# A fused LayerNorm, attention and diffusion kernel on one core: sums by banks at the end, degrees and y earlier at the seam

## The reference

```python
h = jnp.maximum(_layernorm(x, axis=-1), 0.0)
deg = jnp.clip(adj.sum(axis=1), 1.0)
dis = deg ** (-0.5)
diffusion = (dis[:, None] * adj * dis[None, :]) @ h - h
norms = jnp.maximum(jnp.linalg.norm(h, axis=-1), COS_EPS)
sim = h @ h.T / (norms[:, None] * norms[None, :])
attn = jax.nn.softmax(beta * sim * adj, axis=1)
out = x + diffusion + jax.nn.sigmoid(alpha) * (attn @ h - h)
```

## Time and profile before

| | |
|---|---|
| median of 3 runs | 1929.85 us (1928.91 to 1930.41) |
| the profiled execution's own time | 1930.2 us |
| its span, first to last instruction | 1928.3 us |
| mean granted TensorE clock | 0.995 of full |
| TensorE matmul busy | 1829.0 us, 95% of the span |
| VectorE, ScalarE, GpSimd busy | 1222.3, 1307.6 and 1269.9 us |
| the seam: TensorE idle from the last attention sum to the first diffusion matmul | 9.35 us |
| the end: last diffusion matmul at 1918.1, end of the span at 1928.3 | 10.2 us |

### The profile page before, as it was taken

How to read it: one execution, slowest core, us unless ns; L and a number is a source line. 1 busy time by engine, 2 the same in 40 slices (tenths; PEclk the granted TensorE clock), 3 DMA queues, 4 the chain that set the end, 5 groups by cost and what they waited for, 6 DMA issues and landing times.

```text
span 1928.3 us, 44739 instructions
## 1 busy us (share of the span) xinstructions
PE 1829.0 (95%) x19602; PEld 1410.2 (73%) x19602; DVE 1222.3 (63%) x1376; ACT 1307.6 (68%) x1262; POOL 1269.9 (66%) x792
## 2 busy tenths in 40 slices
PE   0499999999999999999999999999997999999997
PEld 0366777777777777777777777777776888888887
DVE  6877787778778777877777787787775210111110
ACT  7688898889889888988988898898886000000000
POOL 3099999999999999999999999999881000000000
PEclk9999999999999999999999999999998999999999
DMA  9639887777888876788887678888217754645520
GB/s 177 96 64 140 102 107 104 91 99 95 101 105 104 103 99 91 100 99 107 100 109 101 89 100 100 106 100 109 61 45 302 246 188 160 207 165 196 176 99 12
DMA packets 188311, 229.38 MB, mean 119 GB/s; under 512 B 9300, under 2 KB 164948, under 8 KB 183380
## 3 DMA queue, kind: packets, MB, share of 16 engines
q0 software_dynamic: 135168, 67.13, 44.8%
q1 hardware_dynamic: 24916, 144.71, 20.2%
q10 hardware_dynamic: 28032, 14.69, 3.0%
HBM read 352.32 MB, written 75.50 MB: 222 GB/s over the span
## 4 chain that ended last, share of the span: by engine, by line
PE 86%; POOL 6%; ACT 3%; DVE 2%; issue 2%; DMA 0%; SPq 0%; POOLq 0%; DVEq 0%; ACTq 0%
PE cos_ps L656 30%; PE cos_ps L715 12%; PE top_ps L715 12%; PE top_ps L686 11%; PE top_ps L690 11%; PE top_ps L688 10%; POOL ustage L275 6%; ACT arena L317 1%; ACT xe L341 0%; PE cos_ps L642 0%; DMA asb<-x_in 0%; DVE ustage L504 0%; POOL hlo L266 0%; DVE ptmp L475 0%; ACT xe L325 0%
## 5 line engine op out<-in xcount | busy, mean ns | idle before, releaser
L275 POOL TENSOR_TENSOR ustage<-xe,ustage 128x1024 f16<-128x1024 f32 x512 | 1095.7, 2144 | 153.0 <-ACT xe L398 148.4
L570 DVE TENSOR_TENSOR xe<-cos_ps,arena 128x1024 f32<-128x1024 f32 x512 | 626.9, 1224 | 286.4 <-PE cos_ps L656 185.0
L394 ACT ACTIVATE ustage<-xe,ebias,ab 128x1024 f16<-128x1024 f32 x512 | 635.4, 1241 | 132.2 <-DVE xe L570 130.8
L686 PE MATMUL top_ps<-h,ustage 128*128 128x129 f16 x4096 | 719.9, 220 | 3.9 <-POOL ustage L275 3.9
L690 PE MATMUL top_ps<-h,ustage 128*128 128x129 f16 x4096 | 719.8, 220 | 0.0
L688 PE MATMUL top_ps<-hlo,ustage 128*128 128x128 f16 x4096 | 719.2, 219 | 0.0
L398 ACT ACTIVATE xe<-xe,ebias,ab 128x1024 f32<-128x1024 f32 x512 | 628.5, 1228 | 3.3 <-POOL ustage L275 2.2
L686 PEld LDWEIGHTS top_ps<-h,ustage 128*128 128x128 f16 x4096 | 401.0, 98 | 72.3 <-POOL ustage L275 12.2
L688 PEld LDWEIGHTS top_ps<-hlo,ustage 128*128 128x128 f16 x4096 | 401.0, 98 | 57.0
L690 PEld LDWEIGHTS top_ps<-h,ustage 128*128 128x128 f16 x4096 | 401.1, 98 | 0.0
L545 DVE TENSOR_REDUCE top_ps<-arena 128x8 f32<-128x1024 uint16 x256 | 311.7, 1217 | 0.0
(11 more groups left out here) (89 smaller groups left out, 1017.7 us busy)
## 6 DMA issues: line engine op xcount, KB each, us to landing
arena<-adj_in_dram POOLq DMA_DIRECT2D x256, 256.0 KB, 8.5
at_scratch<-arena SPq DMA_DIRECT2D x128, 512.0 KB, 3.1
arena<-at_scratch SPq DMA_DIRECT2D x26, 2048.0 KB, 8.6
xe<-at_scratch SPq DMA_DIRECT2D x6, 2048.0 KB, 8.6
h_scratch<-arena SPq DMA_DIRECT2D x4, 1024.0 KB, 7.6
arena<-h_scratch SPq DMA_DIRECT2D x1, 4096.0 KB, 13.4
ustage<-h_scratch ACTq DMA_DIRECT2D x16, 256.0 KB, 8.3
ptmp<-x_in ACTq DMA_DIRECT2D x64, 64.0 KB, 7.4
```

What stands on the lines that cost most here:

```text
L275: nc.gpsimd.tensor_tensor(elo[:, n % ES, :], ef[:, n % XS, :], ehi[:, n % ES, :], ALU.subtract).then_inc(elo_done, 1)
L394: nc.scalar.activation(ehi[:, n % ES, :], xm[:, n % XS, :], ACT.Exp, bias=ebias[:, 0:1], scale=ab[:, 1:2]).then_inc(ehi_done, 1)
L570: nc.vector.tensor_tensor(xm[:, n % XS, :], cos_ps[:, n % 2, :], at8[:, m % W, :, n % B], ALU.mult).then_inc(x_done, 1)
L686: nc.tensor.matmul(top_ps[:, bank, col:col + P + 1], head, h1[:, s, 0:P + 1], start=(first and t % 3 == 0), stop=final, skip_group_check=True)
```

## The change

Five edits, in the kernel's own order:

1. VectorE's row sums run ahead of their units. The first 16 units take 12 pieces in place of 8 (also after units 2, 6, 10, 14), and from then on each piece comes eight units earlier than before. sum_bytes comes after unit 54 of a panel, not 62.
2. degrees() stands ahead of sums(UNITS - 6), not sums(UNITS - 1). VectorE clips straight from PSUM (clip_deg, four operations) after its last masked().
3. ScalarE's order at the seam: the root and the eight y groups now stand ahead of the last panel's copy_acc. y32 moves from ustage to ptmp and has two buffers, not four.
4. h_again comes back in two halves of 2 MB, into two row slots as these fall free (after chunks 29 and 30), not in one of 4 MB after the last row sum. The slots of the second phase are renumbered: chunk 0 goes to the one that chunk 31's rows leave, chunks 3 and 4 wait for y groups 4 and 8.
5. In the last chunk of each panel TensorE goes bank by bank (2 output tiles by 16 tiles of y), and counts each bank done (tiles_done). VectorE adds each bank as it comes (4 operations), signals ScalarE's queue after every second bank, and the queue stores a half panel (4 DMAs) each time.

```diff
--- before.py
+++ after.py
@@ -85,7 +85,6 @@
         gate = sb("gate", [P, 1], fp32)
         gate_tmp = sb("gate_tmp", [P, 2], fp32)
         neg_1_gate = sb("neg_1_gate", [P, 1], fp32)
-        deg = sb("deg", [P, TILES], fp32)
...
@@ -130,9 +129,11 @@
         elo = ustage[:, 2048:4096].bitcast(fp16).rearrange("p (s i) -> p s i", s=ES)
 
         y = [uT_hi[:, :].rearrange("p (s k) -> p s k", k=2 * P), uT_lo[:, :].rearrange("p (s k) -> p s k", k=2 * P)]
-        y32 = ustage[:, :].rearrange("p (g i) -> p g i", g=4)
-        h_again = arena[:, 2 * 4096:4 * 4096].rearrange("p (s d) -> p s d", d=P)
-        slots = [arena[:, 4096:8192], arena[:, 0:4096], xe[:, :], arena[:, 8192:12288], arena[:, 12288:16384]]
+        y32 = ptmp[:, :].rearrange("p (g i) -> p g i", g=2)
+
+        h_again = [arena[:, 4096:8192].rearrange("p (s d) -> p s d", d=P),
+                   arena[:, 12288:16384].rearrange("p (s d) -> p s d", d=P)]
+        slots = [arena[:, 8192:12288], arena[:, 0:4096], xe[:, :], arena[:, 4096:8192], arena[:, 12288:16384]]
         slot8 = [s.bitcast(fp8).rearrange("p (w i b) -> p w i b", w=W, b=B) for s in slots]
         slotw = [s.bitcast(u32) for s in slots]
         SL = len(slots)
@@ -185,7 +186,8 @@
         deg_ready = sem("deg_ready")
         deg_root = sem("deg_root")
         dis_ready = sem("dis_ready")
-        h_back = sem("h_back")
+        h_back = [sem(f"h_back{g}") for g in range(2)]
+        tiles_done = sem("tiles_done")
         y_scaled = sem("y_scaled")
         y_ready = sem("y_ready")
         at_loaded = [sem(f"at_loaded{s}") for s in range(SL)]
@@ -212,17 +214,23 @@
                 sp.dma_start(h_dram[:, g * GW:(g + 1) * GW],
                              h32[:, 16 * g:16 * (g + 1), :].rearrange("p s d -> p (s d)")).then_inc(h_kept[g], 16)
 
+            def h_stored(half):
+                sp.wait_ge(h_kept[2 * half], 16)
+                sp.wait_ge(h_kept[2 * half + 1], 16)
+
             for m in range(BLOCKS):
                 w = m % W
                 sp.wait_ge(at_ready, m + 1)
                 sp.dma_start(at_dram[m // W, :, 1024 * w:1024 * (w + 1)], at_words[:, w, :]).then_inc(at_stored[w], 16)
-
+                if m // W in (CHUNKS - 3, CHUNKS - 2) and w == W - 1:
+
+                    half = m // W - (CHUNKS - 3)
+                    sp.wait_ge(rows_summed, 8 * (m // W + 1))
+                    h_stored(half)
+                    sp.dma_start(h_again[half].rearrange("p s d -> p (s d)"),
+                                 h_dram[:, 4096 * half:4096 * (half + 1)]).then_inc(h_back[half], 16)
 
             sp.wait_ge(rows_summed, 8 * CHUNKS)
-            for g in range(CH):
-                sp.wait_ge(h_kept[g], 16)
-            sp.dma_start(h_again.rearrange("p s d -> p (s d)"), h_dram).then_inc(h_back, 16)
-
             for w in range(W):
                 sp.wait_ge(at_stored[w], 16 * CHUNKS)
             for k in range(CHUNKS):
@@ -230,11 +238,15 @@
                     sp.wait_ge(x_done, UNITS)
                 elif k == 2:
                     sp.wait_ge(elo_done, UNITS)
-                elif k == 3:
-
-                    sp.wait_ge(y_scaled, PANELS)
+                elif k >= 3 and k < SL:
+
+                    sp.wait_ge(y_scaled, 4 * (k - 2))
                 if k >= SL:
-                    sp.wait_ge(at_used, k - SL + 1)
+                    before = k - SL
+                    if before % CH == CH - 1:
+                        sp.wait_ge(tiles_done, PT // 2 * (before // CH + 1))
+                    else:
+                        sp.wait_ge(at_used, (CH - 1) * (before // CH) + before % CH + 1)
                 sp.dma_start(slotw[k % SL], at_dram[k]).then_inc(at_loaded[k % SL], 16)
 
         @block.gpsimd
@@ -397,9 +409,8 @@
                     act.wait_ge(elo_done, n - XS + 1)
                 nc.scalar.activation(ef[:, n % XS, :], xm[:, n % XS, :], ACT.Exp, bias=ebias[:, 0:1],
                                      scale=ab[:, 1:2]).then_inc(ef_done, 1)
-            copy_acc(PANELS - 1)
-
-            act.wait_ge(deg_ready, 1)
+
+            act.wait_ge(deg_ready, Q)
             nc.scalar.activation(vb[:, :], va[:, :], ACT.Sqrt).then_inc(deg_root, 1)
 
             def load_base(panel):
@@ -411,23 +422,26 @@
                         act.dma_start(o2[C * q:C * (q + 1), panel % 2, CH * w:CH * (w + 1), :], x_again_v[b, w0 + w, q]
                                       ).then_inc(base_loaded[panel % 2], 16)
 
-            act.wait_ge(h_back, 16)
             act.wait_ge(dis_ready, 1)
             for g in range(PANELS):
-                if g >= 4:
-                    act.wait_ge(y_ready, g - 3)
-                for s in range(PT):
-                    last = nc.scalar.activation(y32[:, g % 4, s * P:(s + 1) * P], h_again[:, g * PT + s, :], ACT.Copy,
-                                                scale=dis[:, g * PT + s:g * PT + s + 1])
+                if g % 4 == 0:
+                    act.wait_ge(h_back[g // 4], 16)
+                if g >= 2:
+                    act.wait_ge(y_ready, g - 1)
+                for t in range(PT):
+                    s = g * PT + t
+                    last = nc.scalar.activation(y32[:, g % 2, t * P:(t + 1) * P], h_again[s // 32][:, s % 32, :], ACT.Copy,
+                                                scale=dis[:, s:s + 1])
                 last.then_inc(y_scaled, 1)
+            copy_acc(PANELS - 1)
 
             act.wait_ge(y_ready, PANELS)
             load_base(0)
             load_base(1)
             for panel in range(PANELS):
-                act.wait_ge(out_ready, panel + 1)
                 w0, b = panel_of(panel)
                 for w in range(2):
+                    act.wait_ge(out_ready, 2 * panel + w + 1)
                     for q in range(Q):
                         act.dma_start(out_v[b, w0 + w, q], o2[C * q:C * (q + 1), panel % 2, CH * w:CH * (w + 1), :]
                                       ).then_inc(out_stored[panel % 2], 16)
@@ -555,11 +569,11 @@
                                         in_=bytesums.rearrange("p (ch a h) -> p a ch h", ch=CH, h=2),
                                         axis=AX.XY, op=ALU.add).then_inc(rowsums_ready, 1)
 
-            def copy_deg():
+            def clip_deg():
                 dve.wait_ge(deg_done, 1)
                 for q in range(Q):
-                    last = nc.vector.tensor_copy(deg[C * q:C * (q + 1), :], deg_ps[C * q:C * (q + 1), q, :])
-                link(last)
+                    nc.vector.tensor_scalar(va[C * q:C * (q + 1), :], deg_ps[C * q:C * (q + 1), q, :], 1.0 / EIGHT, 1.0,
+                                            ALU.mult, ALU.max).then_inc(deg_ready, 1)
 
             def masked(n):
                 m = n // B
@@ -575,28 +589,26 @@
             dve.wait_ge(hlo_ready, 8)
             turn(0)
             copy_uT(3)
-            sum_rows(0, 0)
-            for n in range(UNITS):
-                masked(n)
+
+            piece = 0
+            for n in range(-1, UNITS):
+                if n >= 0:
+                    masked(n)
                 if n % B == 1 and n // B + 1 < BLOCKS:
                     turn(n // B + 1)
-                elif n % B == 3 and n + 1 < UNITS:
-                    sum_rows((n + 1) // 16, 2 * ((n + 1) % 16 // B))
-                elif n % B == 0:
-                    sum_rows(n // 16, 2 * (n % 16 // B) + 1)
-                if n % TILES == TILES - 2:
+                elif (n % B in (0, 3) or n in (2, 6, 10, 14)) and piece < 8 * CHUNKS:
+                    sum_rows(piece // 8, piece % 8)
+                    piece += 1
+                if n % TILES == TILES - 10:
                     sum_bytes(n // TILES)
-
-            copy_deg()
-            link(nc.vector.tensor_scalar(vc[:, :], deg[:, :], 1.0 / EIGHT, None, ALU.mult))
-            nc.vector.tensor_scalar(va[:, :], vc[:, :], 1.0, None, ALU.max).then_inc(deg_ready, 1)
+            clip_deg()
             dve.wait_ge(deg_root, 1)
             refine_root(va[:, :], vb[:, :], vc[:, :])
             nc.vector.reciprocal(dis[:, :], vb[:, :]).then_inc(dis_ready, 1)
             for g in range(PANELS):
                 dve.wait_ge(y_scaled, g + 1)
                 yg = y[g // 4][:, (g % 4) * PT:(g % 4 + 1) * PT, :]
-                y32g = y32[:, g % 4, :].rearrange("p (s d) -> p s d", d=P)
+                y32g = y32[:, g % 2, :].rearrange("p (s d) -> p s d", d=P)
                 link(nc.vector.tensor_copy(yg[:, :, 0:P], y32g))
                 nc.vector.tensor_tensor(yg[:, :, P:2 * P], y32g, yg[:, :, 0:P], ALU.subtract).then_inc(y_ready, 1)
             dve.wait_ge(acc_copied, PANELS)
@@ -613,17 +625,19 @@
                     last = nc.vector.scalar_tensor_tensor(out=o[:, t, :], in0=asb[:, u, 0:P], scalar=gz[:, u:u + 1],
                                                           in1=o[:, t, :], op0=ALU.mult, op1=ALU.add)
                 link(last)
-                dve.wait_ge(at_used, CH * (panel + 1))
-                for part in range(2):
```

(55 more changed lines are left out.)

## The result

The changed kernel takes 1921.04 us (median of 5 runs, 1919.42 to 1921.91) against 1929.85 (5 runs, 1928.65 to 1930.41): ratio 0.9954, interval 0.9939 to 0.9968, so 0.3 to 0.6% faster. Forecast were 1921.2 us, and 8.7 us of gain, in a range of 1919.0 to 1924.3. The profiled execution took 1921.04 us with a span of 1919.1, 9.2 us less than the span before.

The account below looks back on a forecast made before the run. TensorE was taken to bound the kernel except at prologue, seam and end. End 5.0 plus seam 3.7 gave 8.7 us off the 1929.85 median: 1921.2 us, range 1919.0 to 1924.3 for 8 in 10.

Parts of the forecast that it names:

- The end: Behind the last matmul: four sum operations left (gain 3.11 us) and four stores left (gain 1.88), 5.0 us in all.
- The seam: Between attention and diffusion: table load right behind the last exponential, first diffusion matmul at 1465.16 not 1468.84, gain 3.68 us.
- The table load: ScalarE at the seam: load at 1457.02, no 1.4 us drain counted; rival of a wait for exponentials, 3 of the 16%.
- The clock: First diffusion panel: clock falls again, same price (2.11 us before) within a microsecond; rival that the clock is kept, 12%.
- The loop: Attention loop: VectorE waits 2.1 us for chunk 2, covered with 0.4 us to spare; cost 0, bounds 0 and 1.5.
- The order of the matmuls: Each panel's last chunk: bank order costs nothing, bound 27 ns each; rival that same-bank matmuls wait, 30 us slower, 3%.
- Edit 4 at nothing: Reloading h in two halves costs nothing; only at_scratch's stores stand behind them in SP's list, each with 10.6 us of room.

Follow-up runs that it names:

- the run with UNITS - 4: Changed kernel with the degrees' matmuls ahead of sums(UNITS - 4), behind the last cosines, not at UNITS - 6: 1918.86 us, ratio 0.9944.
- the run with the degrees last: Changed kernel with the degrees' matmuls back ahead of the last unit's sums (UNITS - 1): 1921.91 us, ratio 0.9956.
- the fill: Changed kernel with 64 unread matmuls of 128 columns between attention and diffusion: 1918.97 us, ratio 0.9943; with degrees at UNITS - 4 and two store queues too, 1916.32 us.

## Why the prediction was right, point by point

- *The total.* The medians lie 8.81 us apart, 8.7 were forecast. That the time itself was met to 0.2 us is in part luck: single runs of the changed kernel spread over 2.5 us, by causes for which the sum has no term (below), and the two profiles lie 9.2 us apart. What holds is that both terms came at their size, each by itself.
- *The end, 5.0 us.* Right by its steps: 1.25 us of sums (the row says 1.25) and four stores. 5.16 in the profile; with edit 5 alone, ratio 0.9975, 0.9974 expected.
- *The seam, 3.68 us.* Right: 3.76 in the profile, 3.77 in the attention's length without edit 5. Every step on the path was within 0.1 us. What the sum left untold is how it divides: degrees() at its new place gives 1.0 net, because the matmuls hold masked(511) by 1.7 us; the run with UNITS - 4 gives these 1.63 back. I had the price right and did not ask whether a free place was near.
- *The table load.* I counted it as one block behind the last exponential. It was right here because clip_deg was done first (not under ef, where the prediction puts it, but 0.3 us before ef starts); the run with the degrees last showed that the load does not wait for them. The drain of about 1.4 us that the Trainium skill ("ScalarE: Activation LUTs", What ACT_TABLE_LOAD costs) adds is not seen in any run: in the changed kernel the load starts at the 1457.00 at which the last exponential ends, and Sqrt starts 0.02 us behind the load. By the page's figure the first diffusion matmul would have come 1.4 us later than it did.
- *The clock.* The price came as forecast, 57.72 - 55.89 = 1.83 us against 2.11. Windows of the changed kernel, with the granted clock behind the five busy times:

```profile
1463.00:1464.00 1.00, 0.00 (x0) 0.00 (x0) 0.97 (x2) 1.00 (x4) 0.00 (x0) 1.00 1.09 426
1464.00:1465.00 1.00, 0.00 (x0) 0.00 (x0) 0.94 (x1) 1.00 (x5) 0.00 (x0) 1.00 0.85 328
1465.00:1466.00 1.00, 0.92 (x6) 0.78 (x7) 0.68 (x1) 1.00 (x4) 0.00 (x0) 0.70 1.04 442
1466.00:1467.00 1.00, 1.00 (x7) 0.71 (x5) 0.97 (x2) 1.00 (x5) 0.00 (x0) 0.50 0.54 229
...
1468.00:1469.00 1.00, 1.00 (x7) 0.74 (x6) 0.97 (x2) 1.00 (x5) 0.00 (x0) 0.59 0.04 16
```

The clock is full to the end of the gap of 4.3 us. A mean of 0.70 over 1465 to 1466 is 0.4 us at the full 2.4 GHz and 0.6 at 1.2, so it falls at about 1465.4, when the matmuls have been running for 0.3 us. By the same working it rises at about 1468.8. With the degrees at UNITS - 4 the gap is as long, 4.3 us, but the fall lies in it:

```profile
1461.00:1462.00 1.00, 0.00 (x0) 0.00 (x0) 0.98 (x1) 1.00 (x5) 0.00 (x0) 0.73 0.91 360
...
1468.00:1469.00 1.00, 1.00 (x10) 0.81 (x9) 0.97 (x2) 1.00 (x5) 0.00 (x0) 0.86 1.11 229
```

There it falls at about 1461.5, 0.9 us ahead of the first matmul (1462.39), and rises at about 1468.3. What the first panel pays is half the time that its matmuls run at 1.2 GHz: 3.4 us of them in the changed kernel (1.83 us paid), 5.9 us here (3.02 paid), 4.0 us in the kernel before, to about 1472.9 (2.11 paid). In the five profiles with a gap of 4.3 us the price is 1.55, 1.83, 1.83, 2.50 and 3.02 us, so "the same price within a microsecond" held, and that it came out at 1.83 is luck. What places the fall and the rise is not shown. The fall that the prediction takes as its ground, behind the gap at 98 to 100 us, is also not there in every execution: the changed kernel's profile has that gap too, with a granted clock of 1.00 in each window from 98 to 106 and its attention sums 0.06 us apart throughout, where those of the kernel before go from 0.06 to 0.11 us at 100.7. Halving the gap did not keep the clock in any of the five profiles; filling it did, in both that have the fill.
- *The loop, 0.* Right, and near its edge: wait 1.97 us (2.1 forecast), GpSimd not held. In the other profiles of kernels with edit 1 the wait is 1.81 to 3.09 us; at 3.09, 0.48 us came through.
- *The order of the matmuls, 0.* Right: shown by the run with nothing else changed.
- *Edit 4 at nothing.* In the changed kernel's waits no compute engine is held by h_again, and chunks 3 and 4 of the diffusion held nobody: the panels after the first have 55.89 us as before. It was not tried by itself. What the kernel before shows of h's way back:

```profile
1446.04 0.32 SPq L224 DMA_DIRECT2D arena<-h_scratch  x1
...
arena<-h_scratch SPq DMA_DIRECT2D x1, 4096.0 KB, 13.4
```

Its 4 MB had landed at 1446.04 + 13.4 = 1459.4, and the changed kernel's first y group starts at 1460.51. So as an estimate the load as it was would have been in time by about a microsecond, and the two halves gave nothing at the seam.

A part of what divides runs of one kernel lies in the prologue, and it is the clock again. masked(0) starts at 93.13 us in one profile of the changed kernel and at 91.38 in the other, whose span is 1.8 us shorter (1917.3); the first panel is 57.72 in both. One window of each, during the first cosines (the first line from the profile with 93.13, the second from the one with 91.38):

```profile
91.00:92.00 1.00, 1.00 (x4) 0.34 (x3) 0.36 (x1) 0.00 (x0) 0.00 (x0) 0.50 0.00 0
91.00:92.00 1.00, 1.00 (x7) 0.42 (x5) 0.62 (x1) 0.00 (x0) 0.00 (x0) 1.00 0.00 0
```

In the first, TensorE does cosines(0) at half the clock, and VectorE waits 1.77 us for it ahead of masked(0); in the second it has the full clock, and the wait is 0.50. Of the twelve profiles here, eight have the long wait and four the short one. In some profiles, that of the kernel before among them, the granted clock reads 1.00 in this window although the matmuls come at the slower pace, four in it; the pace is the surer sign there. What places the rise of the clock was not tried.

## What to carry to other kernels

Where one engine is saturated for most of the span, look at the places where it is not, and cost each by its own chain: here the seam and the end gave 8.9 of the 9.2 us, the rest was the clock's, and the 1360 us of the attention loop gave nothing. A small piece of work that is moved forward off a latency chain into a saturated stream is paid in full there; put it behind the last instruction that the chain starts from (here, the last cosines). A last stage can run by banks under the matmuls that feed it; the order of the matmuls that this asks for cost nothing here (at most 1.3 ns a matmul). A gap that can't be closed can be filled with matmuls that nobody reads, which saved 1.7 us here.

## What the runs showed of the hardware that was not expected

- The table load ahead of an activation ran before the semaphore wait of that activation: load at 1455.72, Sqrt at 1459.66.
- The granted clock can fall after matmuls have begun again: in the changed kernel it fell 0.3 us into them, behind a gap of 4.3 us in which it was full. With the degrees at UNITS - 4 and the same gap it fell 0.9 us ahead of them. The price of one and the same gap was 1.55 to 3.02 us in five profiles, and 64 matmuls that nobody reads brought it to 0.16.
- The clock's level in the first cosines alone moves the start of the attention by 1.3 us from one execution to the next (VectorE's wait of 1.77 or 0.50 us ahead of masked(0)).
